# First attention layer with a new engine order, row-sliced keys, four x tiles loaded at the start, and pad rows zeroed by GpSimd inside the first expert stage

## What is computed

```
xn = _layernorm(x)
x = x + _L0_attn_ref(xn, ...) + _L0_ffn_ref(xn, ...)   # layer 0
xn = _layernorm(x)
x = x + _L1_attn_ref(xn, ...) + _L1_ffn_ref(xn, ...)   # layer 1

def _L0_attn_ref(x, norm_w, Wq, Wk, Wv, Wo, gate, log_temperature):  # 4 heads of 32, 2 key/value heads
    h = _rmsnorm(x, norm_w);  q, k, v = h @ Wq, h @ Wk, h @ Wv
    q = _l2norm(q);  k = _l2norm(k)                    # per head
    attn = softmax(where(causal, einsum('bhqd,bhkd->bhqk', q, k) * exp(log_temperature), -inf))
    return x + gate * (einsum('bhqk,bhkd->bhqd', attn, v) @ Wo)
```

## Time and profile before

| | |
|---|---|
| median of 3 runs | 1768.06 us (1767.84 to 1770.22) |
| profiled execution, its own time | 1775.95 us |
| its span in the profile | 1774.2 us, mean granted clock 0.95 |
| PE, DVE, ACT, POOL busy over the span | 87%, 67%, 55%, 47% |
| `setup`, from the start to | about 11 us |
| `layer0_attention`, to | about 438 us |
| first group table and expert stage, to | about 621 us |

### The profile page before, as it was taken

The page is one execution under the profiler, slowest core; times in us unless marked ns, Lnnn a source line. Parts: engine busy times, 40 slices in busy tenths (PEclk is TensorE's granted clock), DMA queues, the critical chain, the costliest instruction groups (busy, mean ns, idle before and its releaser), DMA issues. The chain is left out here.

```text
span 1774.2 us, 29893 instructions
## 1 busy us (share of the span) xinstructions
PE 1545.9 (87%) x9488; PEld 819.9 (46%) x9488; DVE 1183.1 (67%) x3112; ACT 974.2 (55%) x1853; POOL 835.1 (47%) x987
## 2 busy tenths in 40 slices
PE   1788888896699918999999999999999999919996
PEld 0344444453699912333333333333333333319996
DVE  3466665654333346789988898988999989414443
ACT  1455555552244402777777776777777777702221
POOL 2566677661400055456655555555566531004443
PEclk9999999998799955999999998999999999959998
DMA  2111111111899911122222122211222211047772
GB/s 68 34 46 45 40 49 49 49 37 46 258 302 305 262 49 51 48 70 73 64 62 58 55 70 68 64 51 54 71 73 69 64 35 37 13 153 249 240 239 72
DMA packets 141520, 165.76 MB, mean 93 GB/s; under 512 B 28010, under 2 KB 114154, under 8 KB 140138
## 3 DMA queue, kind: packets, MB, share of 16 engines
q1 hardware_dynamic: 86628, 70.75, 13.8%
q10 hardware_dynamic: 40912, 62.62, 11.4%
q0 software_dynamic: 13824, 30.47, 5.5%
HBM read 111.93 MB, written 51.30 MB: 92 GB/s over the span
## 5 line engine op out<-in xcount | busy, mean ns | idle before, releaser
L1566 DVE TENSOR_REDUCE c_mx<-c_ps_mx 128x1 f32<-128x512 f32 x1024 | 648.8, 682 | 92.8 <-PE c_ps_mx L1794 89.7
L1472 ACT ACTIVATE c_pt<-c_ps_e 128x512 f32<-128x512 f32 x1024 | 555.9, 603 | 201.0 <-PE c_ps_e L1766 196.5
L1794 PE MATMUL c_ps_mx<-c_kex,c_qst 72*128 72x512 bf16 x1024 | 401.5, 394 | 17.4 <-issue 8.5
L1766 PE MATMUL c_ps_e<-c_qst,c_kex 74*128 74x512 bf16 x1024 | 392.0, 385 | 1.7 <-ACT c_pt L1472 1.6
L1779 PE MATMUL c_ps_v<-c_pt,c_vp 128*32 128x512 f32 x2048 | 276.7, 612 | 1.1 <-ACT c_pt L1472 0.7
L1309 POOL DMA_INDIRECT c_gy<-ys,mt x128 | 124.0, 969 | 284.5 <-POOLq L69 133.1
L1794 PEld LDWEIGHTS c_ps_mx<-c_kex,c_qst 72*128 72x128 bf16 x1024 | 101.3, 99 | 331.5 <-DVE c_mx L1566 226.4
L1022 PE MATMUL f_ps_h<-f_xT,f_w 128*128 128x256 f32 x800 | 195.8, 384 | 0.0
L673 PE MATMUL a_ps_s<-a_qT,a_kz 128*128 128x128 f32 (+3 forms) x512 | 175.3, 461 | 0.0
L510 POOL DMA_INDIRECT xs<-a_xn,a_meta x128 | 127.6, 997 | 100.2 <-DVE a_meta L413 66.0
L583 ACT ACTIVATE a_pt<-a_ps_s,temp 128x1024 f32<-128x1024 f32 (+3 forms) x128 | 112.9, 884 | 74.5 <-PE a_ps_s L676 72.5
(11 more groups left out here) (230 smaller groups left out, 1958.0 us busy)
## 6 DMA issues: line engine op xcount, KB each, us to landing
f_w<-in_we ACTq DMA_DIRECT2D x80, 321.0 KB, 4.5
f_w<-in_we ACTq DMA_DIRECT2D x40, 576.0 KB, 4.1
c_qst<-qparts SPq DMA_DIRECT2D x45, 384.0 KB
f_x<-rows SPq DMA_DIRECT2D x40, 257.0 KB, 3.9
f_x<-xs SPq DMA_DIRECT2D x80, 128.0 KB, 4.5
ys<-f_y ACTq DMA_DIRECT2D x80, 128.0 KB, 4.2
qparts<-c_qp SPq DMA_DIRECT2D x16, 384.0 KB
c_kex<-kparts SPq DMA_DIRECT2D x48, 96.0 KB
```

The costliest lines, as they stand in the source:

```text
L1472: nc.scalar.activation(pt[:, s % 4, hl, :], ps_e[:, ring_bank(p, n)], ACT.Exp, scale=QSCALE).then_inc(exp_done, 1)
L1566: nc.vector.tensor_reduce(mx[:, g % 2, n % 16:n % 16 + 1], ps_mx[:, ring_bank(p, n)], AX, ALU.max).then_inc(mx_done, 1)
L1766: nc.tensor.matmul(ps_e[:, ring_bank(p, n)], kex[:, p, hl, kt * P:(kt + 1) * P], qst[:, p, HL * g + hl, :], start=True, stop=True).then_in ...
L1794: nc.tensor.matmul(ps_mx[:, ring_bank(p, n)], qst[0:SROW, p, HL * g + hl, qt * P:(qt + 1) * P], kex[0:SROW, p, hl, :], start=True, stop=Tr ...
```

## The change

1. `setup` issues four loads of x into `k.x0`, a tile that is kept, the first of them ahead of the weights, the other three behind `w0` and `w1`. The zeroing of `k.pads` on DVE (8224 columns), its ids, and the store of the pad rows leave `setup`. The block that clears `kz` is gone.
2. `layer0_attention` is written anew with plain loops. x and `xn` have four buffers, `prj` and `r2sq` two, `r2` three. `kz` with its four copies becomes `kT` with one copy, and a score product takes 32 partitions of `kT` and of `qT`; the two heads of a `scores(u)` follow each other, then come both masks. Statistics and norms run three batches ahead instead of two.
3. In `expert_ffn` of layer 0 POOL zeroes `pads` after `move_slots`, and SP stores the pad rows behind its last load of rows and ahead of the store of `meta`.

```diff
@@ setup, SP
-                sp.dma_start(w0[:], i["w0cat"]).then_inc(loaded, 16)
-                sp.dma_start(w1[:], i["w1cat"]).then_inc(loaded, 16)
+                for b in range(RX0):
+                    rows = i["x"][b * L:(b + 1) * L, :]
+                    sp.dma_start(k.x0[:, b], rows.rearrange("(t p) d -> p t d", p=P)).then_inc(k.x0_in[b], 16)
+                    if b == 0:
+                        sp.dma_start(w0[:], i["w0cat"]).then_inc(loaded, 16)
+                        sp.dma_start(w1[:], i["w1cat"]).then_inc(loaded, 16)
...
-                sp.wait_ge(dve_made, 1)
-                sp.dma_start(rows2_d[E1 * REG:, :].rearrange("(e p t) d -> p e (t d)", p=P, e=E1),
-                             k.pads[:, E1:].rearrange("p e t d -> p e (t d)")).then_inc(k.spares_out, 16)
@@ setup, DVE
-                nc.vector.memset(k.pads[:], 0.0).then_inc(dve_pads, 1)
@@ layer0_attention, ACT
-                    for head in range(H0):
-                        r = slice(head * DH0, (head + 1) * DH0)
-                        last = nc.scalar.activation(kz[r, p, head, :], ps_t[r, :], ACT.Copy)
-                    last.then_inc(kT_sb, 1)
+                    nc.scalar.activation(kT[:, b % 2, :], ps_t[:], ACT.Copy).then_inc(kT_sb, 1)
@@ layer0_attention, PE
                     for j in range(2):
-                        head = 2 * pr + j
-                        nc.tensor.matmul(ps_s[:, u % 2, j, 0:L - kt * P], kz[:, p, head, kt * P:(kt + 1) * P],
-                                         qT[:, p, kt * P:L], start=True, stop=False)
-
+                        r = slice((2 * pr + j) * DH0, (2 * pr + j + 1) * DH0)
+                        nc.tensor.matmul(ps_s[:, u % 2, j, 0:L - kt * P], kT[r, b % 2, kt * P:(kt + 1) * P],
+                                         qT[r, b % 2, kt * P:L], start=True, stop=False)
+                    for j in range(2):
                         last = nc.tensor.matmul(ps_s[:, u % 2, j, 0:P], k.ident_b[:], k.causal[:], start=False, stop=True)
@@ layer0_attention, POOL (after)
+                for b in range(NB):
+                    scatter(b, 0)
+                    if b + 3 < NB:
+                        norms(b + 3)
+                    scatter(b, 1)
+                    if b + 2 < NB:
+                        factors(b + 2)
@@ layer0_attention, DVE (after)
+                for b in range(NB):
+                    if b >= 1:
+                        normalise(b - 1)
+                    if b + 3 < NB:
+                        statistics(b + 3)
+                    if b >= 1:
+                        add_output(b - 1)
+                    if b + 1 < NB:
+                        heads_rows(b + 1)
+                        choose(b + 1)
+                        slots(b + 1)
+                        keep_sum(b + 1)
+                    if b + 3 < NB:
+                        normal_rows(b + 3)
+                    if b + 2 < NB:
+                        square_sums(b + 2)
@@ layer0_attention, ACT (after), second half of the body
+                    exps(b, 4)
+                    if nxt2:
+                        prj_copy(b + 2, 2)
+                    exps(b, 5)
+                    if nxt2:
+                        prj_copy(b + 2, 3)
+                        squares(b + 2)
+                    if nxt:
+                        qT_copy(b + 1)
+                        odds(b + 1)
+                    exps(b, 6)
+                    if nxt:
+                        kT_copy(b + 1)
+                    exps(b, 7)
@@ expert_ffn, SP and POOL
+                    sp.wait_ge(k.pads_made, 2)
+                    sp.dma_start(rows2_d[E1 * REG:, :].rearrange("(e p t) d -> p e (t d)", p=P, e=E1),
+                                 k.pads[:, E1:].rearrange("p e t d -> p e (t d)")).then_inc(k.spares_out, 16)
                     sp.wait_ge(meta_new, 1)
...
                     move_slots()
+                    nc.gpsimd.memset(k.pads[:], 0.0).then_inc(k.pads_made, 1)
```

More of the change, by code:

```diff
@@ L35 @@
 GRP = 2 * P
+RX0 = 4
 ROW = 2 * D + 1
@@ L451, in _ @@
-                statistics(0, 0)
-                normal_rows(0, 0)
-                square_sums(0, 0)
-                heads_rows(0, 0)
-                choose(0, 0)
-                keep_sum(0, 0)
-                statistics(0, 1)
-                normal_rows(0, 1)
-                slots(0, 0)
-                square_sums(0, 1)
-                bodies(dve, body)
-                normalise(0, NB - 1)
-                add_output(0, NB - 1)
+                    done(dve, base_out[b % 2], 16 * (b // 2))
@@ new lines, in add_output @@
+                    nc.vector.scalar_tensor_tensor(bs[:, b % 2].rearrange("p t d -> p (t d)"), ps_t[:], k.gate[:, 0:1],
+                                                   xs[:, b % 2].rearrange("p t d -> p (t d)"), ALU.mult, ALU.add).then_inc(wo_used, 1)
+                statistics(0)
+                normal_rows(0)
+                statistics(1)
+                normal_rows(1)
+                square_sums(0)
+                statistics(2)
+                heads_rows(0)
+                normal_rows(2)
@@ L524, in _ @@
-                norms(0, 0)
-                factors(0, 0)
-                norms(0, 1)
-                scatter(0, 0, 0)
-                scatter(0, 0, 1)
-                bodies(pool, body)
+                            xs_d, bass.IndirectOffsetOnAxis(ap=meta[:, b % 2, c * NT + t:c * NT + t + 1], axis=0),
+                            xn[:, b % RX, t, :], None).then_inc(scattered[b % 2], 16)
+                norms(0)
+                norms(1)
+                factors(0)
+                norms(2)
@@ L618, in _ @@
-                rows(1)
-                bodies(act, body)
+                        kT_copy(b + 1)
+                    exps(b, 7)
             @block.tensor
@@ L702, in output @@
                     last.then_inc(wo_ps, 1)
-                def body(i, o):
-                    prev, nxt, nxt2, nxt3 = flags(i, o)
-                    for u in range(4):
-                        scores(i, o, u)
-                    if prev:
-                        output(i, o - 1)
-                    values(i, o, 0)
+                for b in range(2):
+                    x_rows(b)
+                    for t in range(NT):
+                        project(b, t)
+                q_columns(0)
@@ new lines, in _ @@
+                k_columns(0)
+                ranks(0)
+                for b in range(NB):
+                    nxt, nxt2 = b + 1 < NB, b + 2 < NB
+                    scores(b, 0)
+                    scores(b, 1)
+                    if nxt2:
+                        x_rows(b + 2)
+                    scores(b, 2)
+                    if nxt2:
+                        project(b + 2, 0)
+                    scores(b, 3)
+                    if nxt2:
+                        project(b + 2, 1)
+                    if b >= 1:
+                        output(b - 1)
+                    values(b, 0)
+                    scores(b, 4)
+                    if nxt2:
+                        project(b + 2, 2)
+                    scores(b, 5)
+                    values(b, 1)
+                    if nxt2:
+                        project(b + 2, 3)
@@ L740, in _ @@
-                q_columns(0, 0)
-                k_columns(0, 0)
-                rows(1)
-                bodies(pe, body)
-                output(0, NB - 1)
+                        k_columns(b + 1)
+                    scores(b, 7)
+                    values(b, 2)
+                    if nxt:
+                        ranks(b + 1)
+                    values(b, 3)
+                output(NB - 1)
 PRO_DVE_A = 11
```

410 lines of the change are left out of this document (161 added, 249 removed).

## The result

The changed kernel takes 1751.62 us (median of 4 runs, 1744.48 to 1757.1), the kernel before 1769.14 us beside it: a ratio of 0.9895, 95% interval 0.9866 to 0.9924. It is faster by 17.5 us. The prediction was 1715 us with a range from 1695 to 1742, so the gain is under a third of the one forecast and the time lies outside the range. The profiled execution took 1750.46 us (span 1748.7), 25.5 us less than that of before; its mean granted clock is 0.918, where before it was 0.95.

The account below looks back on a forecast made before the run. Layer 0's attention was taken as bound by a ring over POOL, DVE and PE, 23.47 us a batch. Savings of 15.1, 28.2, 4.7 and 7.4 made 55.4: 1768.06 - 55.4 + 2.4 = 1715 us, range 1695 to 1742.

Parts of the forecast that it names:

- up to the ranks of batch 1: Layer 0's attention up to batch 1's ranks: they come at 60.4 instead of 75.52, saving 15.1 us.
- the 14 periods to the ranks of batch 15: Attention loop: thirteen periods of 21.3 instead of 23.47 us save 28.2; body 14, at 18.8, saves 4.7.
- the seam: Between layer 0's experts and layer 1: the pad rows' store ahead of `meta` costs 2.4 us, bounds 0 to 8.
- rival 4: Attention loop: PE pauses lower TensorE's clock, period about 30, 13 x 8.7 us more, 1830 us; chance 0.04.
- The first body: Attention loop's first body: from first ranks at about 41.7 to batch 1's at 60.4, partly at the lower pace.
- The loop's mechanism: Attention loop: scatters use slots made a body earlier; waits round PE, DVE and ACT give a 21.3 us period.
- the sixth pair: Score products in the loop body: this pair waits for the fifth's `exps` until 14.2 and ends at 15.1 us.
- The row strips: Loop's 32-partition score products: a pair of 256 columns takes 0.8 us, bounds 0.65 to 1.1, against 1.1 before.
- Rival 2: Attention loop: dear row strips or an unseen wait, period 23.7, 1747 us; chance 0.23 together with Rival 3.
- Rival 3: Attention loop: late DVE slots keep scatters waiting, period 23.5, about 1743 us; chance 0.23 together with Rival 2.
- Rival 1: Attention loop: POOL is the bound, period 19.9 us, kernel about 1696 us; chance 0.13.
- The start: Setup: last weight at about 8.1, first statistics at 11.4 instead of 20.56 (9.2 us earlier), first ranks about 41.7.

Follow-up runs that it names:

- e5b: Changed kernel with score products over all 128 partitions but half the columns, plus four products once ahead of the loop: 1699.85 us.
- e6: Changed kernel with seven idle 32-partition products ahead of the x transposes: 1743.22 us.
- e1: Changed kernel with each score product run over all 128 partitions: 1717.44 us.
- e2: Changed kernel with seven idle full-height products of 96 columns ahead of the x transposes: 1723.07 us.
- e3: Changed kernel with DVE's slots and keep_sum moved to the end of the body: 1689.61 us.
- e7: e3 with the store of the pad rows behind the loads for layer 1: 1691.21 us.
- e9: e3 with the four loads of x issued behind all eight weight loads: 1684.79 us.
- e8: e3 with score products over all 128 partitions: 1711.7 us.

## Why the prediction was wrong

Against the terms of the sum, in us of the profiled executions:

| term | predicted | measured | from |
|---|---|---|---|
| up to the ranks of batch 1 | 15.1 | 10.5 | 75.52 - 65.04 |
| the 14 periods to the ranks of batch 15 | 32.9 | 6.1 | 328.54 - 322.48 |
| from there to the end of the values | 7.4 | 5.6 | 24.7 - 19.1 |
| the seam | -2.4 | -1.3 | 170.77 - 172.09 |
| the rest | 0 | 4.6 | what is left of 25.5, nearly all behind layer 1's first gather |
| sum | 53.0 | 25.5 | |

**The step that failed** is the dismissal of rival 4, at a chance of 0.04: "Against: 11 us of PE pauses in 100 left it at 1.00". That row is right and was read too far. Its products all had 128 partitions; the changed loop's score products have 32, and no row of before has such a product. The prediction says so where it prices them, but not where it judges the clock. e5b shows that the row holds for full-height products with 18% of pauses, none over 1.5 us; e6 shows that it does not hold for 32-partition ones even almost without pauses. The fall costs 3.2 us in ten periods of fourteen, 32 us, and some 2 us in the last (20.29, where e1, at the upper level, takes 18.37). Behind the last ranks the output again runs at the lower level (2.07 us at 394.97), and that stretch takes 19.1 us and not 17.3. Rival 4's price, 8.7 us a body, was too high as well: only 10 us of a body run at the lower level and part of these lies beside DVE's work.

**The first body** was given 18.7 us, "partly at the lower pace", and took 23.3. By the lengths of its products (2.08 us for a score pair of 512 columns at 42.00, the upper level's 0.70 for one of 256 at 56.59) it runs at the lower level for 15 of them; the granted clock column shows 1.00 there, which these lengths contradict. Here too the strips matter. In e1, from the same start, the first full-height pair of 512 columns still takes 3.70 us (at 41.55), the second already 1.94 (at 45.20), and the body 20.80. e5b, with its four products ahead and shorter pairs, takes 16.65 (42.20 to 58.85).

**The loop's mechanism held.** In bodies at the upper level the period is 20.76, predicted 21.3. Counted from the ranks at 304.94 `output` starts after 9.3 (9.4) and the first values after 10.4 (10.5). In e2's body from 212.31 the fifth pair starts after 12.35 (12.4) and takes 0.76 (0.8), PE waits 0.77 for `qT` (about 1), and the k transposes end after 19.2 (19.7). Too long there was the sixth pair. The sum lets it wait for the fifth's `exps` until 14.2 and end at 15.1; it starts after 13.7 and ends after 14.6, because `scores(u)` waits for `exps(u-2)`, so for the fourth's. These 0.5 us are the whole difference of the period. The wait that the sum did not see is the 1.13 us for `a_xn` ahead of `x_rows`, though its own terms had it: they end `normal_rows` at 4.5, and `x_rows` starts after 4.48 (304.94 to 309.42), while the first two pairs end before 3.4. It lies beside DVE's 9.4 us and costs no time by itself, but it is where the clock falls in the changed kernel, and e3, which removes it, removes the fall from the full bodies. With the fall taken away (e2) the kernel takes 1723 us, inside the range and 8 from the forecast.

**The row strips.** They do run side by side: a pair of 512 columns with masks follows the next after 1.27 us (233.88 to 235.15), the full-height pair after 1.94 (e1, 210.57 to 212.51). By the Trainium skill (TensorE: Matmul & The Clock Gate, "Part 3: Packing small matmuls") products in distinct row groups run together, 3.07 times faster for four; the direction agrees, with 1.94 to 1.27 for two and their masks; no run here has four in a row. By the Trainium skill (TensorEngine Tiling (Array Packing), "Key Properties") a change of tiling mode drains TensorE; here that is inside the 1.27 and does not undo the gain. Behind their masks the next strips start after 0.21 us (234.94 to 235.15), full-height products after 0.12 (212.39 to 212.51), so the change back to strips costs some 0.1 us. Rival 2's dear pairs are refuted; the wait that it allows for exists, but costs nothing by itself. That its period of 23.7 and its 1747 us lie nearest to the measured 23.99 and 1751.6 is chance. Rival 3 is refuted, since the scatters don't wait. Rival 1, POOL as the bound, comes true only with DVE's new order (e3, e7, e9).

**The start** was right to 0.4 us at the first statistics and 0.1 at the first ranks, in part by luck: the weights landed at 9.49 and not at 8.1, and from there to the statistics it took 2.3 us and not 3.3. The prediction charged the loads ahead half a microsecond each and did not ask whether the kernel would be better without them; e9 says yes. **The seam** was inside its bounds; the store took 12.1 us to land and cost 1.3 instead of 2.4, and by the other traces anything from nothing to 1.6.

**The rest**, 4.6 us, lies in code that isn't changed, and in the spread of executions. From layer 1's first gather to the end it is 1151.2 us before and 1146.8 after (622.99 and 601.89 to the ends of the spans), and 1142.7 to 1153.0 in the nine other traces. This is also why the profiled execution's gain, 25.5, is above the medians' 17.5: that of before lies 7 us above its median.

**What stays open:** why three full bodies of the changed kernel, and the last full one of the run with 32-partition fillers, stay at the upper level with the same strips; and what beside the strips is needed, since e3's full bodies keep 1.00 with them. The ten slow bodies were counted in one execution. That their number varies would fit the spread of 12.6 us between runs of this kernel and their mean clocks (0.923 in the fastest, 0.916 in the slowest), but only one of them has a trace.

## What to carry to other kernels

When a change makes PE's products smaller in partitions, the clock of the trace before does not vouch for the clock after: price the loop at both levels, and give the lower one a real chance. Read the granted clock by body, not over the span, and compare one instruction in two bodies; a busier PE with a clock under 1.00 is doing the same work more slowly. Beside such products, an engine's order that leaves PE a pause of 1 us "at no cost" can cost three (without them, in e5b, 1.47 us cost nothing), and moving DVE's least urgent work (here slots and `keep_sum`) to the end of the body removed it; and a load issued first is only worth it if somebody waits for it first.

## What the runs showed of the hardware

- Products of 32 partitions and 128 columns of weights did less to keep TensorE at its upper level than full-height ones. With idle strips in the pause (e6) PE was busy 39.23, 38.45 and 38.45 of 40 us from 120 to 240, at a clock of 0.79, 0.80 and 0.85. With full-height products only (e5b) it was busy 32.8 of 40 us at 1.00 in the full bodies.
- They also did less to bring it there: in the first body the lower level lasted 15 us with strips, until 56.6, and with full-height products it ended before the second pair at 45.2 (e1) or within it, by 47.5 (e8).
- With full-height products pauses of 1.47 us (e5b) and 1.77 us (the kernel before, at 261.05) left the clock at 1.00; one of 2.90 us (e5b) was followed by the lower level. With strips 1.13 us was followed by it in ten bodies of the changed kernel and not in three.
- 14 records of full-height idle products, 1.75 us a body, bought 3.2 us a body.
- In the slow bodies of the changed kernel the fall begins at the pause and the upper level comes back within the values of 512 columns, some 10 us later. In e6 it lasts some 10 us in one body and 7 in the next, where it begins 2 us behind the idle strips.
- Eight small loads land within 5.1 us of their first issue (0.81 to 5.92); with four loads of x of 256 KB each among them the last lands at 9.4. Issue alone accounts for 2.5 of the 3.5 us.
